# Mean squares of the first groups as TensorE products with ones, and the hi/lo splits of the feed-forward weights at other slots

## What is computed

```python
out = (x - mean) * rsqrt(var + 1e-5) * weight + bias
out = (out + tanh(cond @ lin_w.T + lin_b)[:, None, :]) * weight + bias       # stage 0
rms = lambda x: x * rsqrt(mean(x * x, axis=-1) + 1e-6)
x = x + a_alpha * attention(a_gamma * rms(x) + a_beta)    # 16 heads of 16, W_q W_k W_v W_o
h = f_gamma * rms(x) + f_beta
x = x + f_alpha * ((silu(h @ gate_w.T) * (h @ hidden_w.T)) @ out_w.T + out_b)  # 1024 hidden
```

## Time and profile before

| | |
|---|---|
| median of 3 runs | 958.8 us (957.88 to 959.99) |
| profiled execution, whole | 958.45 us |
| its span, first to last instruction | 956.4 us |
| busy | PE 920.8, PE weight loads 885.5, DVE 742.4, ACT 636.4, POOL 499.9 us |
| mean granted TensorE clock | 0.996 |
| DMA | 33.75 MB, 35 GB/s on average |

### The profile page before, as it was taken

One profiled execution on the slowest core, in us unless ns is written; L12 is line 12 of the kernel. 1 busy time (PEld: TensorE's weight loads), 2 busy tenths in 40 slices (PEclk: granted clock), 3 DMA queues, 4 the chain that ended last, 5 costly groups with the idle time before them and its releaser, 6 DMA issues.

```text
span 956.4 us, 28592 instructions
## 1 busy us (share of the span) xinstructions
PE 920.8 (96%) x11064; PEld 885.5 (93%) x11064; DVE 742.4 (78%) x1438; ACT 636.4 (67%) x1839; POOL 499.9 (52%) x477
## 2 busy tenths in 40 slices
PE   5668999999999999999999999999999999999998
PEld 5557999999999999999999999999999999998998
DVE  6987787788778778878877887877877787667665
ACT  3656767767776776776676677677668667666432
POOL 3596455555554555555456556555565545543320
PEclk9999999999999999999999999999999999999999
DMA  6200012110021201112121111102101011100000
GB/s 231 69 2 29 13 24 57 24 51 12 20 58 23 57 24 45 15 23 57 24 53 27 23 37 24 57 24 51 31 6 52 24 35 18 19 13 13 13 12 23
DMA packets 40630, 33.75 MB, mean 35 GB/s; under 512 B 10800, under 2 KB 39984, under 8 KB 40496
## 3 DMA queue, kind: packets, MB, share of 16 engines
q1 hardware_dynamic: 40496, 31.93, 13.6%
HBM read 23.37 MB, written 8.55 MB: 33 GB/s over the span
## 4 chain that ended last, share of the span: by engine, by line
PE 90%; DVE 4%; POOL 2%; issue 2%; ACT 1%; DMA 0%; SPq 0%; DVEq 0%; ACTq 0%; POOLq 0%
PE psum L375 18%; PE psum L377 18%; PE psum L376 18%; PE psum L626 6%; PE psum L625 6%; PE psum L624 6%; PE psum L539 5%; PE psum L511 4%; PE psum L555 4%; PE psum L410 2%; PE psum L429 1%; DVE least L790 1%; PE psum L422 1%; POOL probs L1371 0%; DVE row_sum L806 0%
## 5 line engine op out<-in xcount | busy, mean ns | idle before, releaser
L375 PE MATMUL psum<-xf_hi,ffn_hi 128*128 128x256 f32 x1024 | 291.2, 284 | 0.8 <-ACT probsT L1142 0.6
L376 PE MATMUL psum<-xf_lo,ffn_hi 128*128 128x256 f32 x1024 | 288.1, 281 | 0.0
L377 PE MATMUL psum<-xf_hi,ffn_lo 128*128 128x256 f32 x1024 | 287.8, 281 | 0.0
L1134 ACT ACTIVATE probs<-psum,least 128x64 f32<-128x64 f32 x928 | 205.2, 356 | 38.5 <-DVE least L790 37.7
L1371 POOL TENSOR_TENSOR probs<-probs,inv_sum 128x512 f32<-128x512 f32 x128 | 134.6, 1053 | 153.3 <-DVE inv_sum L811 153.3
L375 PEld LDWEIGHTS psum<-xf_hi,ffn_hi 128*128 128x128 f32 x1024 | 192.7, 188 | 1.7 <-issue 1.2
L376 PEld LDWEIGHTS psum<-xf_lo,ffn_hi 128*128 128x128 f32 x1024 | 192.8, 188 | 0.0
L377 PEld LDWEIGHTS psum<-xf_hi,ffn_lo 128*128 128x128 f32 x1024 | 192.7, 188 | 0.0
L1177 ACT ACTIVATE prod_hi<-late 128x512 fp32r<-128x512 f32 x127 | 83.1, 654 | 125.8 <-DVE late L884 125.5
L626 PE MATMUL psum<-prod_hi,ffn_lo 128*128 128x256 f32 x512 | 144.1, 281 | 0.0
L625 PE MATMUL psum<-prod_lo,ffn_hi 128*128 128x256 f32 x512 | 144.1, 281 | 0.0
(11 more groups left out here) (123 smaller groups left out, 2162.0 us busy)
## 6 DMA issues: line engine op xcount, KB each, us to landing
out_t_dram<-x_res SPq DMA_DIRECT2D x31, 256.0 KB, 3.2
xin<-x_dram SPq DMA_DIRECT2D x15, 512.0 KB, 6.7
shift_tok<-shift_rows SPq DMA_DIRECT2D x104, 64.0 KB, 3.3
inv_row<-inv_rows SPq DMA_DIRECT2D x26, 128.0 KB, 4.8
w_raw<-attn_w_dram SPq DMA_DIRECT2D x1, 1024.0 KB, 8.2
x_res<-gate_w_dram SPq DMA_DIRECT2D x1, 1024.0 KB, 10.9
late<-hidden_w_dram SPq DMA_DIRECT2D x1, 1024.0 KB, 12.5
w_raw<-out_w_dram SPq DMA_DIRECT2D x1, 1024.0 KB, 6.4
```

Of the source, the lines that this page charges most:

```text
L375: pe.matmul(out, stat_hi, mov_hi, start=first, stop=False)
L376: pe.matmul(out, stat_hi, mov_lo, start=False, stop=False)
L377: return pe.matmul(out, stat_lo, mov_hi, start=False, stop=last)
L1134: op = act.activation(probs[g % 4][:, h * SEQ:(h + 1) * SEQ], scores[g % 2][:, h // 2, h % 2], ACT.Exp, bias=least[g % 2][:, h:h + 1], sca ...
```

## The change

It does five things. (1) For groups -2 to 2 POOL's sums are gone; TensorE multiplies the squares (as stationary, 128 tokens at a time) with a column of ones, two products accumulated over the feature halves, so the mean squares arrive as columns; DVE adds the epsilon straight from PSUM, and this one operation signals. ACT's squares wait for the product instead of the sum. From group 3 on all is as before, with semaphore counts shifted. (2) Splits of chunks 5, 6, 7 go to slot 10, 8 and 1 to slot 11, 3 to slot 12, and 9, 10, 11 from slots 12, 13, 14 to 13, 14, 15. (3) The merge of block 2's statistics goes from the end of slot 3 to the end of slot 4. (4) DVE's low part of the attended values goes before `scale_f` in slot 10; ACT's `square_f` goes between the two exponentials in slot 8 and ahead of the copy of the keys in slot 12. (5) POOL's `split_lo_a` goes before both normalised probabilities in slot 2 and behind both in slot 10 (it was between them, and stays so in slot 6).

```diff
 LAST_STEP = FFN_STEPS - 1
 LATE_TURNS = (BATCH - PSEQ - 1, BATCH - 1)
-SPLITS = {-3: (0, 2), -2: (4,), 1: (5,), 3: (7,), 5: (6,), 6: (8,), 9: (1,), 11: (3,), 12: (9,), 13: (10,), 14: (11,)}
+SPLITS = {-3: (0, 2), -2: (4,), 10: (6, 5, 7), 11: (8, 1), 12: (3,), 13: (9,), 14: (10,), 15: (11,)}
 SPLIT_ORDER = [c for chunks in SPLITS.values() for c in chunks]
...
 QUAD = 32
 ROW_FROM = 6
+SUMMED_FROM = 3
 
...
         ident = sb("ident", [P, P])
         warm = sb("warm", [P, 2])
+        ones = sb("ones", [P, 1])
         minus_half = sb("minus_half", [P, TILES])
...
         def is_group(grp):
             return turns_a(grp) or is_part(grp - 2)
+
+        def summed(grp):
+            return grp >= SUMMED_FROM
+
+        def sum_no_a(m):
+            return m - 1 - SUMMED_FROM
+
+        def sum_no_f(m):
+            return m + 3 - SUMMED_FROM
 
...
                 mm.then_inc(x_turned, 1)
 
+            def sum_to_column(n, squares):
+                for i in range(2):
+                    for kt in range(KT):
+                        mm = pe.matmul(norm_bank[:, 2 * n + i:2 * n + i + 1], squares[:, kt, i * P:(i + 1) * P], ones[:],
+                                       start=kt == 0, stop=kt == KT - 1)
+                return mm
+
+            def square_columns(grp):
+                if turns_a(grp):
+                    pe.wait_ge(squared_a, grp + 3)
+                    mm = sum_to_column(0, squares_a)
+                if is_part(grp - 2):
+                    pe.wait_ge(squared_f, grp - 1)
+                    mm = sum_to_column(1, squares_f)
+                mm.then_inc(ms_mm, 1)
+
             def turn_squares(grp):
+                if not summed(grp):
+                    square_columns(grp)
+                    return
                 if turns_a(grp):
-                    pe.wait_ge(sq_sum_a, grp + 3)
+                    pe.wait_ge(sq_sum_a, sum_no_a(grp + 2))
                     for i in range(2):
                         mm = pe.transpose(norm_bank[:, i * P:(i + 1) * P], square_sum_a[:, i * P:(i + 1) * P], ident[:])
                 if is_part(grp - 2):
-                    pe.wait_ge(sq_sum_f, grp - 1)
+                    pe.wait_ge(sq_sum_f, sum_no_f(grp - 2))
                     for i in range(2):
...
                     dve.wait_ge(inv_spread, grp + 2)
                 cols = norm_cols(grp, 1)
+                if not summed(grp):
+                    dve.tensor_scalar(mean_sq[:, cols], norm_bank[:, cols], RMS_EPS, None, ALU.add).then_inc(ms_read, 1)
+                    return
                 dve.tensor_reduce(square_mean[:, cols], norm_bank.rearrange("p (n c) -> p n c", c=P)[:, cols], AX_X, ALU.add
...
                     make_residual(grp + 2)
                 if s == FFN_AT:
-                    merge_stats((grp + 3) // 2, (grp + 3) // 2 + 2)
+                    merge_stats(3, 5)
                 if j == 2 and s >= 0 and is_part(grp + 2):
...
                 if j == 2 and is_part(grp - 2) and not wide(s):
                     scale_f(grp - 2)
+                if j == 2 and is_part(grp - 1) and wide(s):
+                    attended_lo(grp - 1)
                 if j == 2 and is_part(grp - 2) and wide(s):
                     scale_f(grp - 2)
-                if j == 2 and is_part(grp - 1) and wide(s):
-                    attended_lo(grp - 1)
                 for g in (s, s + 1):
...
                 if grp % 2 == 0 and 2 <= (grp + 4) // 2 < NBLK:
                     token_stats((grp + 4) // 2, j)
-                    if j == 3 and grp != 2:
+                    if j == 3 and grp > 2:
                         merge_stats((grp + 4) // 2, (grp + 4) // 2 + 2)
+                if s == PSEQ:
+                    merge_stats(2, 4)
                 for c in SPLITS.get(s if s < 0 else s - 1, ()) if s != 0 else ():
...
                 act.wait_ge(res_made, 2 * m + 2)
                 if m >= 1:
-                    act.wait_ge(sq_sum_a, m)
+                    act.wait_ge(ms_mm, m)
                 act.activation(squares_a[:], res_part(m), ACT.Square, scale=ROOT_D).then_inc(squared_a, 1)
...
                 act.wait_ge(y_tok, n + 1)
                 if n == 0:
-                    act.wait_ge(sq_sum_a, ROW_FROM)
+                    act.wait_ge(sq_sum_a, sum_no_a(ROW_FROM - 1))
                 if n >= 4:
...
             def square_f(m):
                 act.wait_ge(resid_made, m + 1)
-                if m >= 1:
-                    act.wait_ge(sq_sum_f, m)
+                if m >= 1 and summed(m + 1):
+                    act.wait_ge(sq_sum_f, sum_no_f(m - 1))
+                elif m >= 1:
+                    act.wait_ge(ms_mm, m + 4)
                 act.activation(squares_f[:], res_part(m), ACT.Square, scale=ROOT_D).then_inc(squared_f, 1)
...
                 if s == FFN_AT:
                     square_a(grp + 2)
+                    square_f(grp - 2)
                     keys_out(grp + 1)
-                    square_f(grp - 2)
                 if s % 2 == 0 and is_seq(s):
...
                     if wide(s) and j == 2 and is_part(grp - 1):
                         attended_hi(grp - 1)
+                    if wide(s) and j == 0 and is_part(grp - 2):
+                        square_f(grp - 2)
                     if wide(s + 1):
...
                 if j == 0 and s >= 0 and is_part(grp + 2) and not PSEQ <= s <= FFN_AT and not row_part(grp + 2):
                     square_a(grp + 2)
-                if j == 0 and is_part(grp - 2) and wide(s):
-                    square_f(grp - 2)
                 if j == 2 and is_part(grp - 1) and not wide(s):
...
 
             def inverse_rms(grp):
-                pool.wait_ge(ms_out, grp + 3)
+                if summed(grp):
+                    pool.wait_ge(ms_out, grp - SUMMED_FROM + 1)
+                else:
+                    pool.wait_ge(ms_read, grp + 3)
                 cols = norm_cols(grp, 1)
...
             def sum_squares_a(m):
                 pool.wait_ge(squared_a, m + 1)
-                if m >= 1:
-                    pool.wait_ge(ms_mm, m)
                 pool.tensor_tensor(square_sum_a[:], squares_a[:, 0], squares_a[:, 1], ALU.add).then_inc(sq_sum_a, 1)
...
 
             pool.memset(warm[:], 1.0 / D)
+            pool.memset(ones[:], 1.0)
             pool.memset(minus_half[:], -0.5).then_inc(consts_set, 1)
...
                     apply_beta_a(1)
                     split_lo_a(1)
-                if j == 0 and 0 <= s < FFN_AT:
-                    sum_squares_a(grp + 2)
-                    if is_part(grp - 2):
-                        sum_squares_f(grp - 2)
                 if j == 2 and 0 <= s < FFN_AT:
...
                 for g in (s, s + 1):
                     if s % 2 == 0 and is_seq(g) and wide(g):
+                        if s == 2 and g == s:
+                            split_lo_a(grp + 2)
                         normalise_probs(g)
-                        if g == s and j == 2:
+                        if s == 6 and g == s or s == 10 and g == s + 1:
                             split_lo_a(grp + 2)
                 if s == FIRST_SLOT or s == FIRST_SLOT + PSEQ:
-                    sum_squares_a(grp + 2)
                     if s == FIRST_SLOT:
                         half_rstd(1)
                     apply_gamma_a(grp + 2)
```

## The result

The changed kernel takes 972.38 us in the median (971.12 to 973.52), the kernel before 959.14 us beside it: a ratio of 1.014, with an interval of 1.0127 to 1.0153. The forecast was 967, its range 961 to 971. The direction and the three waits came as forecast. The loss of 13.2 us is 4.9 us larger than the 8.35 of the sum, and the time lies 1.4 us above the range.

What follows compares the result with a forecast made beforehand. TensorE, 96% busy, was taken to bound the kernel, any stall from slot 13 on being lost. Stalls 9.25 net, plus clock 3.0, minus early gain 3.9, gave 8.35 us on the 956.4 span: 967 us measured time, range 961 to 971.

Steps and rivals of the forecast that it cites:

- the three waits: TensorE stalls before down(1), down(2), down(3) in slots 14 to 16, behind late out splits: 4.0, 2.9 and 2.85 us.
- What bounds the kernel: Up to slot 12 Pool, DVE or ACT can matter; from slot 13 any microsecond TensorE stands still is lost.
- the two short waits of slot 17: TensorE's waits before the queries and the turn of squares, claimed to vanish behind the stalls: -0.5 us.
- The lower of two readings for down(2): Slot 15's DVE chain without meeting Pool: 2.9 us of stall, against 4.4 us if it meets Pool.
- The slow clock: Half clock behind each of the three stalls: 1.0 us each, 3.0 in all (0 to 4.9).
- The upper bound of 4.9: Most that half clock behind the three stalls could cost in all; each was said to cost 0 to 1.7 us.
- The early gain: Start-up through slot 12, to the turn of squares: 3.9 us earlier, bounds 2.0 and 6.0.
- Eight instructions with one moving column: TensorE's products with ones in the early slots: 0.75 us at full clock, 1.4 us at half.
- The new add: DVE's small add reading PSUM for groups -2 to 2, replacing reduce and old add: 0.17 us.
- the products are dear: Rival for slots 1, 5 and 9: 0.21 us an instruction at full clock, early gain 1 us, 970 and more; chance 0.10.
- the clock stays: Rival: stalls come in dense work but without a slow clock, 961 to 964 us; chance 0.18.
- the early chain gives over 11 us: Rival in slots 2 to 12: chain shortens by more than 11.2 us, kernel faster, 956 with 12 us; chance 0.07.

Runs made afterwards that it cites:

- e11: Kernel before the change with only chunk 9's split moved from slot 12 to 13, made ahead of chunk 10: 964.15 us, ratio 1.0057.
- e2: Kernel before the change with only the splits of chunks 9, 10, 11 moved to slots 13, 14, 15: 972.37 us, ratio 1.0136.
- e4: e3 with 20 more unused products ahead of the wait of the turn of squares in slot 13: 967.56 us, ratio 1.0094.
- e1: Changed kernel with the splits of chunks 9, 10, 11 back in slots 12, 13, 14: 958.05 us, ratio 0.9993.
- e3: Changed kernel with 32, 24 and 20 unused TensorE products filling the waits before the three down products: 971.76 us, ratio 1.0136.
- e7: e1 with the slot 11 splits of chunks 6, 5, 7 put ahead of ffn_split_lo, where DVE waited: 958.82 us, ratio 0.9996.
- e8: e7 with ten unused TensorE products ahead of the turn of squares in slot 13: 958.83 us, ratio 0.9996.
- e9: e1 with slot 12's exponentials ahead of the copy of the keys and its merge at the slot's end: 957.54 us, ratio 0.9991.
- e5: Changed kernel's moves with e1's splits, but Pool's sums and the transposes kept as before the change: 958.46 us, ratio 0.9995.

## Why the prediction was right or wrong

**What bounds the kernel: right.** From slot 13 on a wait of TensorE reaches the end: e11 shows it with one wait, e2 with three. What is given back are the two short waits of slot 17 that the sum had at 0.5 us: 0.67 in after, 0.8 in e11.

**The three waits: right.** 4.0, 2.9 and 2.85 were forecast, 3.93, 3.05 and 2.70 measured, 9.68 for 9.75 (10.16 by the starts). Each was built from rows of before, although no row showed it: the split is the last operation of DVE in the slot whose product needs it, and the chain behind TensorE's last input gives the wait. The lower of two readings for down(2) held: L902 and L780 didn't meet Pool there (0.68 and 0.48 us).

**The slow clock: the step that failed, by size and by count.** The sum put it at 3 x 1.0 us, because part of a slow stretch would fall into the wait. Hardly any did: the half level came at most 0.3 us before the matmuls, the third time behind them, and 1.50, 1.42 and 1.44 us were lost. This makes 4.4 for 3.0. The 1.7 of rows 8, a loss of clock, is a little above it: at the half level the matmuls' starts lie 0.21 us apart for 0.12, which is less than twice. The fourth stretch was not in the sum at all. Rows 7 showed a wait of 1.53 us before the turn of squares without a lower clock; that the early gain makes it longer (all of TensorE's work ahead comes sooner than the exponentials do) was not asked. It went to 2.53 us, and 1.53 were lost behind it. Together 5.9 for 3.0, and e4 confirms it by taking all four away. (The upper bound of 4.9 should have been 5.1 by its own 1.7 each, and four stretches pass both.)

**The early gain: too large by 1.8 us.** 3.9 us were forecast at the turn of squares, 2.12 measured. The stations of the step, in after (the numbers of before stand in rows 5, 6 and 7):

```profile
45.70 0.39 PE L386 MATMUL psum<-xn_hi,w_hi 128*128 128x256 f32 x1 [0.48 <-ACT k_heads L1133]
...
63.97 0.94 PE L428 MATMUL psum<-ones,squares_a 128*128 128x1 f32 x8
64.78 1.03 PE L428 MATMUL psum<-ones,squares_f 128*128 128x1 f32 x8
65.84 0.16 DVE L873 TENSOR_SCALAR mean_sq<-psum 128x4 f32<-128x4 f32 x1 [0.64 <-PE psum L428]
66.08 1.03 POOL L1346 TENSOR_TENSOR mean_sq<-mean_sq,minus_half 128x4 f32<-128x4 f32 x1
```
```profile
84.09 1.75 ACT L1171 ACTIVATE probs<-psum,least 128x64 f32<-128x64 f32 x8
```

The queries came at 45.70 for a forecast 45.35, the inverse at 66.08 for 65.0, the exponentials of slot 12 at 84.09 for 82.6. So the gain fell short a little from station to station: by 0.35, 0.73, 0.41 and 0.28 us. (At the queries the sum carried 2.55 us on, where its own 45.35 for 47.66 gives 2.31.) Two terms show in the trace. Eight instructions with one moving column took 0.81 and 0.96 us by the distance of starts (63.97, 64.78, and 65.74 for the next operation), where 0.75 was taken; eight transposing ones with 128 moving columns take 0.96 too (L569, 94.75 to 95.71), so one moving column saves little or nothing. The Trainium skill, "TensorE: Matmul & The Clock Gate", section "LDWEIGHTS (loading the stationary operand)", has the load depend on the stationary columns alone and gave 0.86 by estimate; the trace agrees. Next, the merge of slot 12, which stood there before as well, now meets Pool: two of its small operations took about 1 us each, where the one between them took 0.15. Before, the same two took 0.17 and 0.16 us (L727, L730, at 84.94 and 85.10).

```profile
84.09 0.97 DVE L757 TENSOR_SCALAR mean<-merge 128x4 f32<-128x4 f32 x1
84.97 0.15 DVE L758 SCALAR_TENSOR_TENSOR merge<-merge 128x4 f32<-128x4 f32 x1
85.05 1.02 DVE L760 TENSOR_SCALAR merge<-merge 128x4 f32<-128x4 f32 x1
```

It ends at 86.26, behind the exponentials' end (85.84), so that the row sums start 0.3 us late: this is the last shortfall, 4.38 us from the exponentials to the turn for 4.09. The rest of the 1.8 us has no row of its own, and nothing of this was run by itself. The new add took 0.16 us for a forecast 0.17.

The 2.12 us are also one pair of executions. With the changed start the turn came at 88.47 (after), 88.93 (e1) and 90.41 (e3), with the old one at 90.59 (before), 90.85 (e2) and 92.46 (e11), each with other slow stretches ahead of it. The means lie 2.0 us apart, so the size fits, but no single pair settles it.

**What the early gain was worth: less than its own size.** The prediction carried 3.9 us to the end unchanged. Of the 2.12 measured, 1.53 went back in the slow stretch behind the turn. e1 fits: its turn comes 1.66 us earlier than before's and its down(0) 0.13 (93.78 for 93.91), and with all of the early edits and none of the late splits its ratio is 0.9993. Both terms of the sum erred towards the better, by (5.9 - 3.0) + (3.9 - 2.1) = 4.7 us, and the waits by 0.2: 967.15 + 4.9 = 972.1, for 972.38 measured. That this comes so close is partly luck, as the start differs by more than that from execution to execution.

**The rivals.** That the products are dear (0.21 us an instruction): no, their starts lie about 0.10 apart (eight from 63.97 to 64.78). That the clock stays: no. That the early chain gives over 11 us: no, 2.1. The bounds of the sum gave 960.1 to 973.3, and the time lies in them; the range was cut by 0.9 us at the lower end and by 2.3 at the upper one, although the price of the clock had a row (1.7 us each, rows 8) and the 1.0 that was taken lay well under it.

**Open.** What length of standing still brings the half level isn't settled (next section). That the early gains expected of e7 and e8 were lost at the port shared with Pool is an explanation that fits the rows; no run took Pool's operations away.

## What to carry to other kernels

An operation at the end of an engine's list for a slot, whose reader stands in the same slot on another engine, makes the reader wait for the whole chain ahead of it; built from the durations of the rows, the three waits here came out within 0.2 us. A wait in dense work is best given the full price that a half-clock stretch has elsewhere in the same trace, as most waits of 2.5 us and more had it here, and an earlier gain can lengthen a wait and so bring one more such stretch. Before work is moved into a gap of DVE, look at what Pool does in the same gap: three splits took 4.53 us there for 1.87.

## What the runs showed of the hardware

**The price of a drop of the clock.** In dense work it was nearly the same each time: 1.42 to 1.53 us by the distances of starts in the four of after, 1.61 in that of e11. With twenty 128-column products in the gap before the turn of squares and 0.3 us of wait left there was none (e4); with ten, and 1.4 us left, there was (e8).

**When it drops isn't a matter of one idle time.** Waits of 1.01 us (e3) and 1.41 us (e8) were followed by it, one of 2.45 us (e9) was not. Nor does it come with the wait itself: in e3 the clock fell 1.7 us after TensorE had gone on working, in after once 0.6 us after. In after TensorE was busy 0.80 of the 4 us from 28, and the clock stayed at its full level:

```profile
28.00:32.00 4.00, 0.80 (x6) 1.00 0.00 0
32.00:36.00 4.00, 3.47 (x56) 1.00 0.00 0
```

**The same kernel draws a different number of drops.** In the ten executions of e9 the mean granted clock was 0.998 at the shortest time, 956.38 us, and 0.993 at the longest, 960.29; in those of e5 it was 0.998 at 956.51 and 0.993 at 959.80. One stretch that costs 1.7 us of clock is 0.0018 of the span, so by this estimate the 0.005 between them are about three stretches more, which covers the 3.9 us. In the profiled executions all slow stretches lie ahead of 140 us; where they lay in the others isn't on record. Such a spread can hide an early gain of 1 to 2 us, as those that were tried here.

**Small operations of DVE beside Pool.** Operations on 128x4 elements took 0.97 and 1.02 us in the merge of slot 12, about as long as the two of Pool that ran beside them (1.04 each, at 84.00 and 85.00), and 0.15 us between them. The add on 128x4 elements that reads PSUM took 0.16 us although one of Pool ran beside it (L1409, to 66.02).
